# Two-layer transformer kernel: key-value, chunk, router, down and future products at other slots, elu's minimum on POOL

## What is computed

```python
x = x + L0_attn(layernorm(x)) + L0_ffn(layernorm(x))   # softmax attention, 16 heads; fp4-quantized gated FFN
x = x + L1_attn(layernorm(x)) + L1_ffn(layernorm(x))   # below

# L1_attn: linear attention, heads of 8
q = elu(rope(q) * SCALE) + 1.0
k = elu(rope(k) * SCALE) + 1.0
for t in range(N):                      # the kernel does this in chunks of 128 tokens
    kv = kv + k[t] (x) v[t];  ks = ks + k[t]
    out[t] = (q[t] @ kv) / max(q[t] . ks, 1e-6)

# L1_ffn: top 2 of 4 experts by softmax scores, plus one shared expert, all computed for all tokens
y = sum_e comb[:, e] * down_e(silu(gate_e(x)) * up_e(x)) + down_s(silu(gate_s(x)) * up_s(x))
```

## Time and profile before

| | |
|---|---|
| median of 3 runs | 2140.8 us (2138.5 to 2142.2) |
| profiled execution, device time | 2139.74 us |
| its span, first to last instruction | 2137.9 us |
| busy: PE / PEld | 1939.8 us (91%) / 1267.2 us (59%) |
| busy: DVE / ACT / POOL | 1544.0 (72%) / 1376.8 (64%) / 1148.3 us (54%) |
| chain that ended last, by engine | PE 53%, ACT 15%, DVE 12%, POOL 7%, issue 7%, SP queue 3%, DMA 2% |
| granted TensorE clock, mean | 0.975 of full speed |

### The profile page before, as it was taken

The page is one execution under the profiler, slowest core; times in us unless marked ns, Lnnn a source line. Parts: engine busy times, 40 slices in busy tenths (PEclk is TensorE's granted clock), DMA queues, the critical chain, the costliest instruction groups (busy, mean ns, idle before and its releaser), DMA issues.

```text
span 2137.9 us, 50103 instructions
## 1 busy us (share of the span) xinstructions
PE 1939.8 (91%) x17353; PEld 1267.2 (59%) x17353; DVE 1544.0 (72%) x5224; ACT 1376.8 (64%) x3861; POOL 1148.3 (54%) x1800
## 2 busy tenths in 40 slices
PE   3788999999999998999999899999999999998968
PEld 1455665656566574656657566565656657565646
DVE  7557778687776868777686777868777676866745
ACT  1777585676857667585766758576685856757531
POOL 4685374745637465473746547374563746555220
PEclk7779999999999999999999999999999999999989
DMA  5011011110101111010111201111010111101010
GB/s 140 18 22 33 4 29 32 28 34 19 35 10 28 33 29 32 12 38 15 29 33 28 33 4 32 28 29 34 23 33 9 28 33 24 33 12 35 4 31 6
DMA packets 180848, 59.44 MB, mean 28 GB/s; under 512 B 147835, under 2 KB 178163, under 8 KB 180595
## 3 DMA queue, kind: packets, MB, share of 16 engines
q1 hardware_dynamic: 180595, 56.23, 12.3%
HBM read 14.22 MB, written 4.19 MB: 9 GB/s over the span
## 4 chain that ended last, share of the span: by engine, by line
PE 53%; ACT 15%; DVE 12%; POOL 7%; issue 7%; SPq 3%; DMA 2%; ACTq 0%; DVEq 0%; POOLq 0%
PE ps L1132 10%; PE ps L1268 8%; PE ps L1203 7%; PE ps L1213 6%; PE ps L1146 5%; ACT ring L954 5%; PE ps L1122 4%; ACT pb L963 3%; SPq L428 3%; PE ps L1253 3%; DVE ring L584 3%; PE ps L1191 2%; DVE lin L616 2%; PE ps L1111 2%; DMA qkT<-kx 2%
## 5 line engine op out<-in xcount | busy, mean ns | idle before, releaser
L851 POOL TENSOR_SCALAR ring<-ring,row_rcp,tau_row 128x128 f32<-128x128 f32 (+3 forms) x1024 | 629.6, 623 | 700.8 <-DVE row_rcp L591 700.8
L954 ACT ACTIVATE ring<-ring,neg_max 128x128 f32<-128x128 f32 (+3 forms) x1024 | 570.7, 558 | 504.0 <-DVE neg_max L584 499.5
L1132 PE MATMUL ps<-identf,ring 128*128 128x128 f32 x2560 | 378.7, 287 | 9.9 <-POOL ring L851 7.6
L963 ACT ACTIVATE pb<-ps 128x512 f32<-128x512 f32 x640 | 348.6, 584 | 29.6 <-PE ps L1132 25.5
L1132 PEld LDWEIGHTS ps<-identf,ring 128*128 128x128 f32 x2560 | 279.4, 143 | 83.2 <-issue 40.1
L584 DVE CUSTOM_DVE_ANT_1 ring<-ps,bias_t 128x384 f32<-128x384 f32 (+1 forms) x496 | 286.9, 614 | 55.0 <-PE ps L1122 47.8
L1268 PEld LDWEIGHTS ps<-ed_t,h 128*128 128x128 f32 (+1 forms) x1920 | 256.5, 192 | 98.3 <-issue 94.8
L1268 PE MATMUL ps<-ed_t,h 128*128 128x128 f32 (+1 forms) x1920 | 272.7, 278 | 0.0
L1203 PE MATMUL ps<-xn1T,eg_t 128*128 128x512 f32 (+1 forms) x480 | 256.6, 616 | 2.1 <-DVE h L633 2.1
L1213 PE MATMUL ps<-xn1T,eu_t 128*128 128x512 f32 (+1 forms) x480 | 256.6, 616 | 1.1 <-DVE h L640 0.9
L616 DVE TENSOR_TENSOR lin<-ps,tri_t 128x512 f32<-128x512 f32 x256 | 164.7, 685 | 127.8 <-PE ps L1179 127.8
(11 more groups left out here) (154 smaller groups left out, 2822.0 us busy)
## 6 DMA issues: line engine op xcount, KB each, us to landing
x_t<-x SPq DMA_DIRECT2D x16, 256.0 KB, 3.1
x<-x SPq DMA_DIRECT2D x16, 256.0 KB, 2.9
o_rows<-o_stack SPq DMA_DIRECT2D x256, 16.0 KB
out<-x SPq DMA_DIRECT2D x16, 256.0 KB, 2.8
qkT<-qx SPq DMA_TRANSPOSE x192, 2.4
qkT<-kx SPq DMA_TRANSPOSE x192, 2.4
bias_t<-bias SPq DMA_DIRECT2D x1, 1536.0 KB, 8.0
eg_t<-eg SPq DMA_DIRECT2D x1, 860.0 KB
```

What stands on the lines that cost most here:

```text
L851: pool.tensor_scalar(e, e, row_rcp[:, m % 2, r:r + 1], tau_row[:, i, HG * g + r:HG * g + r + 1], ALU.mult, ALU.add).then_inc(p_ok.sem, 1)
L954: act.activation(e, e, ACT.Exp, bias=neg_max[:, n % 2, r:r + 1], scale=-1.0, accum_out=row_sum[:, n % 2, r:r + 1]).then_inc(exp_ok.sem, 1)
L963: act.activation(pb[:, c % NPB, :], bank(turn_bank(q)), ACT.Relu).then_inc(t_taken[q % 2].sem, 1)
L1132: last = pe.transpose(o[:, r * P:(r + 1) * P], ring_of(i, r)[:, k * P:(k + 1) * P], idf)
```

## The change

The tables put several items of layer 1 at other slots: the three key-value products from 29, 29 and 31 to 33, 47 and 53; the turned queries from 30 to 46; the router's first full slot from 31 to 37; the second and third expert's down products from 42 and 48 on to 44 and 49 on; the chunk products from 40, 42, 46 and 53 to 40, 44, 48 and 52. The slots at which an expert's output is accumulated get a table of their own, in which the first three are 43, 48 and 53 in place of 39, 46 and 52. Future values go from slots 61 and 63 of a sequence's softmax frame to slots 1 and 3 of the next frame. Elu's minimum goes from VectorE to POOL, right behind the rope addition of the same tile, and its buffer gets four tiles in place of three. ACT's copy of a chunk product of an even slot now stands between the two exponentials, ahead of the stored probabilities, instead of at the slot's end.

```diff
-TURN_H, FUTURE_V, FUTURE_Y = (ATT + 11, ATT + 13, ATT + 13, ATT + 15), ATT + 61, ATT + 63
+TURN_H, FUTURE_V, FUTURE_Y = (ATT + 11, ATT + 13, ATT + 13, ATT + 15), ATT + 65, ATT + 67
-KV, TURN_Q32 = (L1 + 29, L1 + 29, L1 + 31), L1 + 30
+KV, TURN_Q32 = (L1 + 33, L1 + 47, L1 + 53), L1 + 46
-INTRA = (L1 + 40, L1 + 42, L1 + 46, L1 + 53)
+INTRA = (L1 + 40, L1 + 44, L1 + 48, L1 + 52)
-ROUTER = L1 + 31
+ROUTER = L1 + 37
-DOWN1 = [GATE1[3 * e + 2] + 4 for e in range(NE - 1)] + [L1 + 65]
+DOWN1 = [L1 + p for p in (35, 44, 49, 56, 65)]
+ADD_EXPERT = [L1 + p for p in (43, 48, 53, 60, 69)]
...
-                if 0 <= p - QKV1 - 2 < T:
-                    elu_low(b, p - QKV1 - 2)
...
-                    if p == DOWN1[e] + 4:
+                    if p == ADD_EXPERT[e]:
                         accumulate(b, e)
...
+            def elu_low(b, t):
+                pool.wait_ge(qk_ok[1].sem, qk_ok[1].at(b, t + 1))
+                pool.tensor_scalar(elu_m[:, t, :], qk[:, t, :], 0.0, None, ALU.min).then_inc(elum_ok.sem, 1)
...
                     if p == QKV1 + ROPE1[t] + 1:
                         rope_add(b, 1, t)
+                        elu_low(b, t)
...
-                if p in INTRA:
-                    g = INTRA.index(p)
-                    turned(("intra", b, g), nd[:, g, :])
+                if p in INTRA and p % 2:
+                    store_intra(b, INTRA.index(p))
...
                 if has(f) and s % 2 == 0:
                     exp_with_sum(f, s)
+                for b, p in plan.beside(f, s):
+                    if p in INTRA and p % 2 == 0:
+                        store_intra(b, INTRA.index(p))
                 for blk in plan.blocks(f, s):
                     store_probs(*blk)
```

More of the change, by code:

```diff
@@ L244, in build @@
         nd = sb("nd", [P, G, L])
-        elu_m = sb("elu_m", [P, 3, 2 * D])
+        elu_m = sb("elu_m", [P, T, 2 * D])
         qT32 = sb("qT32", [P, L])
@@ L641, in hidden @@
                                          op0=ALU.mult, op1=ALU.mult).then_inc(g_taken[1].sem, 1)
-            def elu_low(b, t):
-                dve.wait_ge(qk_ok[1].sem, qk_ok[1].at(b, t + 1))
-                if t >= 3:
-                    dve.wait_ge(elu_ok.sem, elu_ok.at(b, t - 2))
-                dve.tensor_scalar(elu_m[:, t % 3, :], qk[:, t, :], 0.0, None, ALU.min).then_inc(elum_ok.sem, 1)
             def elu_high(b, t):
                 dve.wait_ge(elue_ok.sem, elue_ok.at(b, t + 1))
-                dve.scalar_tensor_tensor(out=qk[:, t, :], in0=qk[:, t, :], scalar=0.0, in1=elu_m[:, t % 3, :],
+                dve.scalar_tensor_tensor(out=qk[:, t, :], in0=qk[:, t, :], scalar=0.0, in1=elu_m[:, t, :],
                                          op0=ALU.max, op1=ALU.add).then_inc(elu_ok.sem, 1)
@@ L977, in tanh_gate, with store_intra @@
                 act.activation(tanh_t[0:rows, k % 2, 0:n], bank(G0)[0:rows, 0:n], ACT.Tanh, scale=0.5).then_inc(tanh_ok.sem, 1)
+            def store_intra(b, g):
+                turned(("intra", b, g), nd[:, g, :])
             def elu_exp(b, t):
                 act.wait_ge(elum_ok.sem, elum_ok.at(b, t + 1))
-                act.activation(elu_m[:, t % 3, :], elu_m[:, t % 3, :], ACT.Exp).then_inc(elue_ok.sem, 1)
+                act.activation(elu_m[:, t, :], elu_m[:, t, :], ACT.Exp).then_inc(elue_ok.sem, 1)
             def norm(b, layer, src, dst):
```

## The result

The change made the kernel slower: 2232.5 us (median of four runs, 2230.0 to 2234.8) against 2141.5 us for the kernel before on the same chip (2138.5 to 2142.9), a ratio of 1.0427 [1.0408, 1.0445]. The forecast was 2195 us with a range of 2155 to 2216: the sign was right, 53.7 us were forecast, and 91 came. The profiled execution took 2229.97 us with a span of 2228.2, 90.3 more than before.

What follows compares the result with a forecast made beforehand. The transposes' chain bounds each frame's first half, TensorE's work the second. Terms -0.2 + 1.7 + 1.3 + 1.2 + 0.2 - 0.7 = +3.5 us in 15 frames, plus 1.2 in the last, gave 2195 us, range 2155 to 2216.

Steps and rivals of the forecast that it cites:

- The transposes bound the first half: Slot 20 to the first `lin` of slot 35: the DMA transposes' chain sets its end, so only -0.2 us a frame.
- The stall of slot 44: Slot 44: TensorE's second turned block waits for ACT's copy behind an exponential that waits for VectorE; +1.7 us a frame.
- The work that moved into the full half: Slots 45 to 53: down tiles +1.3 us, turned queries and key-value products +1.2, chunk products ahead of blocks +0.2.
- the clock as a rival: Ahead of the first `lin`: TensorE's clock falls in 12 frames more, 18 us on top, 2213 us; chance 0.22.
- its own sign of being wrong: Listed signs: first half shorter by over 0.8 us, second half as long as before, or granted clock falling often.
- -0.7 us for the future values: Across the frame's end: next value products start some 1.2 us earlier, part returns in slots 1 and 3; net -0.7 us.
- the rival that was to lengthen the frame by 0.4 us: First half: POOL's minima at 0.9 us each use up the cover, up to 0.4 us a frame, 2201 us; chance 0.05.

Runs made afterwards that it cites:

- u_copy: The changed kernel with ACT's copy of even chunk products moved ahead of the exponential of the slot's first score tile; 2189.9 us, ratio 1.022.
- u_router: The changed kernel with the router's steps back at slots 28 to 37 and the first accumulation back at slot 39; 2187.0 us, ratio 1.022.
- x_all: The changed kernel with ACT's copy ahead of the exponential, and router, first accumulation, key-value products and turned queries back at earlier slots; 2160.7 us, ratio 1.009.
- v_gate: The kernel before with POOL's minimum, and the fifth gate at slot 34, not 35; 2210.9 us, ratio 1.032.
- w_downfv: The kernel before with first down products one slot earlier and future values at slots 25 and 33, without POOL's minimum; 2134.1 us, ratio 0.996.
- b_fv: The kernel before with the two future-value products at slots 25 and 33, not 61 and 63; 2138.4 us, ratio 0.9994.
- u_fv: The changed kernel with the two future-value products back at slots 61 and 63; 2237.0 us, ratio 1.045.

## Why the prediction was wrong in size

**Right, and shown.** The transposes bound the first half: 1.75 us less work of TensorE, and 0.2 us of time. The second half takes 402.67 - 335.12 = 67.55 us in frame 2, where some 67 were forecast. The stall of slot 44 has the cause, the place and nearly the size forecast (+1.7, measured +2.0), and goes when either half of its cause goes (u_copy, u_router). The work that moved into the full half costs its length there: 2.7 forecast, 2.6 measured in slots 45 to 53, of which u_kv returns 0.9 and x_all leaves 1.7. Slots 54 to 57 cost 0.5 us more, which the forecast had not; with the key-value products and turned queries back (u_kv) it is gone. That it is the third of the products was expected, but no run moves it alone.

**The step that failed first: the clock as a rival instead of a consequence.** The prediction looked for the fall ahead of the first `lin` and held against it that waits of 1.7 us there had seldom brought one. It put a new wait of 2.3 us into the full half in its own sum, and didn't ask what TensorE's clock would do behind that one. So the term for the clock in the sum was nothing, and its own sign of being wrong came true: "a granted clock that fell often". In the changed kernel each of the 18 falls in frames 1 to 14 starts between 1 us ahead of the end of a wait of 2.2 to 2.3 us and 1.4 us behind it, in slots 28 or 44. Those behind slot 44 cost 1.2 us a frame, 17 us in the 14 frames; u_copy takes the wait away and nine of the ten falls with it, and v_gate brings both at another place. The falls of slot 28 lie where TensorE has room: the first half takes 26.24 us on average with them and 26.47 before. The Trainium skill (TensorE: Matmul & The Clock Gate, Part 1) says that idle gaps between bursts bring the half clock back; these rows agree. They don't show a wait's length as the whole cause: u_router's six falls follow waits of 0.8 us, the one left in u_copy a wait of 0.6, w_downfv waits 1.5 us in slot 30 of every frame and has no fall there, and of the 28 waits of 2.2 to 2.3 us in frames 1 to 14 of the changed kernel 10 are followed by none. What tells these apart stays open.

**The step that failed second: -0.7 us for the future values.** "The next frame's value products can start some 1.2 us earlier" is true, they started 1.0 us earlier in b_fv, but the step took TensorE's order for what bounds the stretch across the frame's end. The turned blocks behind POOL's scalings start 8.9 to 9.0 us after slot 62 either way. The term measured -0.2 (u_fv).

**A term mis-sized, and hidden.** POOL's minimum was taken at 0.58 us, the row of a scaling of the same size. The group by shape of the changed kernel (count, then shortest, median and longest ns) says:

```profile
L833 POOL TENSOR_SCALAR elu_m<-qk x64: 843/847/898, 182.0 to 2154.3; 128x256 f32<-128x256 f32 x64
```

That is close to the 0.9 of the rival that was to lengthen the frame by 0.4 us. It did not: on POOL's timeline of frame 2 the low stack, ahead of which POOL idled 2.06 us before, now starts without a pause,

```profile
320.60 2.03 POOL L848 TENSOR_SCALAR ring<-ring,row_rcp,tau_row 128x256 f32<-128x256 f32 x3
322.60 0.43 POOL L840 TENSOR_TENSOR qx<-qk,qx 128x128 f16<-128x128 f32 x1
```

322.60 - 309.33 = 13.27 us after slot 20, against 697.50 - 684.07 = 13.43 before. The cover was used to its end, and the 0.2 us saved on VectorE ahead of it remain (0.17 with the minimum alone, b_min). What the minimum costs is a wait in slot 28, in the half that has room; the forecast had put the longer wait in slot 32, where it is 0.8. The wait ahead of the first `lin` is 21.4 / 14 = 1.5 us, a little below the 27.0 / 16 = 1.7 of before, not above it as forecast. Both means hold the last frame, which has no softmax work (6.2 and 5.0 us); without it they are 1.2 and 1.5, so the waits against which the prediction set its rival were shorter than the 1.7 that it names.

**Sum.** Forecast +3.5 us a frame. Measured +4.7 where the clock stays up (0.3 more in the stall, 1.0 more from slot 54 to the next frame's slot 20, where -0.7 stood, and 0.1 less in slots 45 to 53), and 1.2 for the clock: 5.9, less the 0.3 that the kernel before lost to its own falls.

**A version that beats both.** w_down: the kernel before with the first expert's down products one slot earlier, 0.6% faster than before. The change as a whole moved work the other way, out of the half with room into the half without.

## What to carry to other kernels

Cut a frame into stretches and ask of each what ends last before pricing a move: work costs its length where TensorE is full, and less in a stretch that another engine bounds, but not nothing by rule: the future values in the first half of the kernel before made it 0.4 us longer, and with the down tile as well 1.1. A saving ahead of a stretch that another chain bounds comes back as a wait in it. A wait that a change puts into a full stretch is to be priced with what TensorE's clock does behind it; here that was 1.2 us on top of 2.0. And before a copy frees a bank that TensorE waits for, look at what stands ahead of it in its engine's queue: one exponential there, itself waiting for a late VectorE, cost, with the clock, about as much as all the work that was moved into the full half (43 us, and 15 x 2.6 = 39).

## What the runs showed of the hardware that was not expected

POOL takes 847 ns for a minimum of 128x256 with a constant and 578 ns for a scaling of the same size by two columns. The granted clock falls to 0.5 around the end of a single wait of 2.2 to 2.7 us or shortly behind it, in slots 28 and 30 of the half with room and in slots 35 and 44 of the half that is otherwise full, and in one kernel behind waits of 0.8 us; it does not do so behind every such wait. The fall lasts 3.4 us as a rule (6.8 at times) and costs up to 1.9 us where TensorE is full. And where the fall sits moved from slot 44 (10 frames, then 3) to slot 28 (8, then 13) when only work in other slots was moved (u_kv), with both waits still there.
